# A four-layer graph network on one core: gathered rounds stand behind other dense units of a step

## The reference, cut to what matters

```
def sage_conv(x, src, dst, Wl, bl, Wr):
    msg = x[src]
    agg = jax.ops.segment_sum(msg, dst, num_segments=N_NODES)
    deg = jax.ops.segment_sum(jnp.ones((src.shape[0], 1), x.dtype), dst, num_segments=N_NODES)
    agg = agg / jnp.maximum(deg, 1.0)
    return agg @ Wl.T + bl + x @ Wr.T
...
edge_index = jnp.stack([src, dst])
x = _layernorm(x + _L0_gnn_ref(...), axis=-1)      # gat
x = _layernorm(x + _L1_gnn_ref(x, edge_index))     # dev: sums of x[src] and of its square
x = _layernorm(x + _L2_gnn_ref(x, edge_attr_64, src, dst, ...))   # gine
x = _layernorm(x + _L3_gnn_ref(x, edge_index, ...))               # sage1 .. sage4
```

## Time and profile before

| what | value |
|---|---|
| median of 3 runs | 10336.57 us (10336.55 to 10338.63) |
| the profiled execution's own time | 10338.73 us |
| its span | 10336.9 us, granted PE clock 0.819 of full speed |
| busy share of the span | PE 68%, PE weight loads 50%, DVE 46%, POOL 44%, ACT 18% |
| HBM | 1337.9 MB read, 225.0 MB written |

### The profile page before, as it was taken

One profiled execution on the slowest core, in us unless ns is written; L12 is line 12 of the kernel. 1 busy time (PEld: TensorE's weight loads), 2 busy tenths in 40 slices (PEclk: granted clock), 3 DMA queues, 4 the chain that ended last, 5 costly groups with the idle time before them and its releaser, 6 DMA issues.

```text
span 10336.9 us, 260758 instructions
## 1 busy us (share of the span) xinstructions
PE 7025.2 (68%) x70494; PEld 5117.6 (50%) x70495; DVE 4776.3 (46%) x12912; ACT 1865.3 (18%) x3800; POOL 4554.0 (44%) x4467
## 2 busy tenths in 40 slices
PE   5888778778735666666778866666676454555677
PEld 4666556556522221113454545665675454444676
DVE  4555555555468877774443333333232332222333
ACT  2333333332211334551000000000000000000000
POOL 3777656555410000004661045435554765553754
PEclk7899888888868988998889977777777776667788
DMA  3444333333310122335556665665566676556676
GB/s 68 95 94 92 83 89 83 82 80 72 74 49 25 75 87 112 137 135 172 165 172 183 179 207 194 208 217 178 204 223 207 220 273 212 199 201 228 205 253 228
DMA packets 973370, 1566.22 MB, mean 152 GB/s; under 512 B 499841, under 2 KB 621441, under 8 KB 966402
## 3 DMA queue, kind: packets, MB, share of 16 engines
q1 hardware_dynamic: 485762, 1244.14, 34.2%
q0 software_dynamic: 150016, 196.43, 9.4%
q10 hardware_dynamic: 337280, 122.87, 4.6%
HBM read 1337.91 MB, written 225.00 MB: 151 GB/s over the span
## 4 chain that ended last, share of the span: by engine, by line
PE 38%; issue 18%; DVE 15%; POOL 12%; DVEq 9%; DMA 6%; ACT 2%; ACTq 0%; SPq 0%; POOLq 0%
PE ps_turn L977 15%; POOL ARENA L662 12%; PE ps_out L824 6%; PE ps_turn L932 4%; DMA ARENA<-counts 3%; PE ps_pair L824 2%; DMA ARENA<-edge_attr 2%; PE ps_turn L797 2%; DVE ARENA L1766 2%; DVE ARENA L1764 2%; PE ps_turn L735 1%; PE ps_out L739 1%; DVEq L1771 1%; PE ps_pair L859 1%; PE ps_out L1014 1%
## 5 line engine op out<-in xcount | busy, mean ns | idle before, releaser
L977 PE MATMUL ps_turn<-ARENA 128*128 128x192 bf16 (+2 forms) x28812 | 2722.3, 261 | 708.7 <-DVE DSUM L1916 322.7
L977 PEld LDWEIGHTS ps_turn<-ARENA 128*128 128x128 bf16 x28812 | 2286.0, 105 | 1134.9 <-issue 824.1
L662 POOL DMA_INDIRECT ARENA<-table_sage,idx x1920 | 1866.9, 972 | 1510.0 <-issue 993.2
L662 POOL DMA_INDIRECT ARENA<-table_gat,idx x1568 | 1728.8, 1103 | 1054.9 <-DMA idx<-src_r 557.2
L932 PE MATMUL ps_turn<-ARENA 128*128 128x392 bf16 (+1 forms) x4204 | 1058.5, 356 | 676.3 <-DVE ARENA L1766 375.4
L662 POOL DMA_INDIRECT ARENA<-table_dev,idx x480 | 469.8, 979 | 1671.3 <-ACT idx L1177 1527.9
L1764 DVE TENSOR_SCALAR ARENA<-ARENA 128x784 bf16<-128x784 f16 (+1 forms) x2102 | 1007.2, 479 | 357.1 <-issue 230.9
L932 PEld LDWEIGHTS ps_turn<-ARENA 128*128 128x128 bf16 (+1 forms) x4204 | 332.4, 100 | 1402.3 <-issue 1357.7
L662 POOL DMA_INDIRECT ARENA<-table_gine,idx x480 | 469.8, 979 | 945.4 <-issue 691.3
L1159 ACT ACTIVATE ARENA<-ps_turn 128x784 f32 x784 | 646.1, 824 | 1077.5 <-PE ps_turn L932 1077.1
L1916 DVE TENSOR_REDUCE DSUM<-ps_turn 128x64 f32<-128x192 f32 (+2 forms) x686 | 263.6, 384 | 1171.0 <-PE ps_turn L977 1074.4
(11 more groups left out here) (303 smaller groups left out, 6913.7 us busy)
## 6 DMA issues: line engine op xcount, KB each, us to landing
ARENA<-counts SPq DMA_DIRECT2D x1764, 448.0 KB
counts<-ARENA SPq DMA_DIRECT2D x49, 3136.0 KB, 9.0
ARENA<-counts SPq DMA_DIRECT2D x588, 224.0 KB
ARENA<-dst_b SPq DMA_DIRECT2D x393, 256.0 KB
ARENA<-edge_attr ACTq DMA_DIRECT2D x392, 128.0 KB
ARENA<-table_sage,idx POOLq DMA_INDIRECT x1920
ARENA<-table_gat,idx POOLq DMA_INDIRECT x1568
nodes_dev<-table_rows ACTq DMA_DIRECT2D x14, 672.0 KB
```

Of the source, the lines that this page charges most:

```text
L662: pool.indirect_dma_start(ps["buf"][:, s, c, 0:ps["row"]], None, ps["table"][:, :], bass.IndirectOffsetOnAxis(idx[:, s, c:c + 1], 0)).then ...
L977: last = pe.matmul(ps_dense[half][:, 0:n], RING[:, b, :], XP[:, b, :], start=(b == PIECE_AT[pieces[0]]), stop=(j == pieces[-1] and b == PI ...
```

## The change

`begin_step` loads two numbers for a step in place of one: a `gain` and a first value of `share`. For a step with n rounds behind step 0, `gain` is (n-1) sixths (in 16.16) and `share` begins at 1 minus `gain`, so that the first round stands behind the first unit and the last behind the last, the others evenly between; a step with one round has it behind its first unit. Step 0 keeps its equal shares. The units behind which a round stands (counted from 0):

| step | rounds | before | after |
|---|---|---|---|
| 0 | 3 | 2, 4, 6 | 2, 4, 6 |
| 1 | 3 | 2, 4, 6 | 0, 3, 6 |
| 2 to 5 | 2 | 3, 6 | 0, 6 |
| 6 | 1 | 6 | 0 |

```diff
+LATER_SHARE = (1 << 16) // (TB - 1) + 1
...
-        GAINS = sb("GAINS", [P, STEPS], I32)
+        SHARES = sb("SHARES", [P, STEPS, 2], I32)
...
             gain, share, base, _, upto = turns
-            eng.reg_load([gain], GAINS[0:1, bass.ds(b, 1)])
-            eng.reg_mov(share, 0)
+            eng.reg_load([gain, share], SHARES[0:1, bass.ds(b, 1), :].rearrange("p a k -> p (a k)"))
             eng.reg_mov(base, upto)
...
-                gain = small[:, 2, 0:STEPS]
-                step(ve.tensor_tensor(gain, TARGETS[:, 1:STEPS + 1], TARGETS[:, 0:STEPS], ALU.subtract))
-                step(ve.tensor_scalar(gain, gain, float(TURN_SHARE), None, ALU.mult))
-                step(ve.tensor_copy(GAINS[:, :], gain))
+                rounds, gain, start = (small[:, q, 0:STEPS] for q in (2, 3, 4))
+                step(ve.tensor_tensor(rounds, TARGETS[:, 1:STEPS + 1], TARGETS[:, 0:STEPS], ALU.subtract))
+                step(ve.tensor_scalar(gain, rounds, -1.0, 0.0, ALU.add, ALU.max))
+                step(ve.tensor_scalar(gain, gain, float(LATER_SHARE), None, ALU.mult))
+                step(ve.tensor_scalar(start, rounds, 1.0, float(1 << 16), ALU.min, ALU.mult))
+                step(ve.tensor_tensor(start, start, gain, ALU.subtract))
+                step(ve.tensor_scalar(gain[:, 0:1], rounds[:, 0:1], float(TURN_SHARE), None, ALU.mult))
+                step(ve.memset(start[:, 0:1], 0.0))
+                step(ve.tensor_copy(SHARES[:, :, 0], gain))
+                step(ve.tensor_copy(SHARES[:, :, 1], start))
```

## The result

| | before | after |
|---|---|---|
| median of 7 runs each, on one chip | 10339.89 us (10336.55 to 10352.51) | 10387.46 us (10375.98 to 10408.45) |
| the profiled execution's span | 10336.9 us | 10394.3 us |

The ratio is 1.0047, with a 95% interval of 1.0036 to 1.0058: the changed kernel is slower by 47.6 us. The forecast was 10380 us.

The account below looks back on a forecast made before the run. Waits bound the kernel, no engine being busy over 68%; rounds end at least 41 to 42 us apart by gathers. Six passes +37.0 and `dev`'s load +6.3 make +43 on 10336.6: 10380 us, range 10357 to 10425 (0.68).

Parts of the forecast that it names:

- F: From a step's last round's end to the next step's first round's end: 41 us by gathers, 56.2 to 69.4 elsewhere.
- W: Six units in a row after a step's first round: 48.7 to 51 us by pass, sized from step 6 before.
- the two-round steps: Steps 2 to 5: F + 1.1 + W + 12.9, 103.7 to 134.4 us by pass; they lose, most in `sage2`.
- the last round in `dev`: Round ending a two-round step, its gathers already in hand: 12.9 us.
- Step 1: Three rounds, three units apart: F + 2 x 41.5, 124.0 to 152.4 us by pass; a gain in every pass.
- Step 6: One round behind unit 0: F + 1.1 + W, 90.8 to 121.5 us by pass.
- `dev`'s load: `XP` reload at the end of `dev`'s first half loses its covering round; PE waits 15 us bare, net +6.3 us.
- The cover is needed: One-hots made inside first rounds delay PE 5.5 us in `gine`, `sage3`, 4.5 in `sage1`; rival, not needed: 10287 us, chance 0.14.
- given back in `sage2`: Rival: after waiting, PE runs six units 6.7 us faster per step, total 10340; chance 0.12 shared with another place.
- The rounds stand where the change puts them: Rival: rounding of `share` puts the first round behind unit 1, about 10340; chance 0.12 shared with the wait given back.
- DVE's node work holds the gathers back: Rival: rounds waiting for gathers beside node work end later than 41 us, up to 10623 in all; chance 0.06.
- the 8 us ahead of `more_hots`: Sign of being right: behind unit 0, `more_hots` some 8 us after the unit's first sum, four one-hots between.

Follow-up runs that it names:

- one unit later: Against the kernel before: rounds of steps 2 to 5 behind units 1 and 6, other steps as before; 10349.35 us, ratio 1.0011.

## Why the prediction was right

**F was right in size, and in two of the six passes by luck.** The first round of a step ends 41.9, 68.8, 54.5, 40.8, 57.7 and 41.4 us after the last one (`dev` to `sage4`, means of six steps); forecast were 41, 69.4, 56.2, 41, 57.6 and 41. In `sage2` the cause is shown by halving the gathers, in `gine`, `sage1` and `sage3` by doubling the one-hots. In `dev` and `sage4` the prediction let the round end with its gathers "whatever PE does". But PE waits there for DVE, 69.3 and 65.1 us for `tile_hots` beside 4.1 and 11.4 for gathered rows; half the gathers take only 1.0 and 1.7 us off F, and four more one-hots add 2.8 and 2.0. With half the gathers no first round there waits for rows in steps 2 to 5, so DVE's node work and one-hots take some 40.9 and 39.7 us by themselves; that this lies next to 41 was not foreseen. In `gine`, `sage1` and `sage3` the sum held two errors that cancelled: a round without waits lasts 12.6 to 13.0 us there and not 11, and a first round is longer than that by 3.3, 2.2 and 3.5 us and not 5.5, 4.5 and 5.5. The 3.47 us that the earlier trace rows show ahead of `more_hots` are not spent a second time.

**W was mis-sized.** Six units in steps 2 to 5 take 48.9, 53.9, 52.7, 48.5, 49.0 and 53.3 us; forecast were 50, 51, 51, 48.7, 48.7 and 51. The term came from step 6, where no gathers run in `gine` and `sage3`. Beside gathers it is longer, and with half of them it falls back to 51.5, 51.5, 47.0, 46.9 and 51.4 in `gine` to `sage4` (`dev` stays at 49.2). Over four steps the six differences make some 24 us, and the two-round steps exceed the forecast by 24.0; the last round in `dev`, 14.1 us where 12.9 were taken, adds some 5, and `sage1`'s shorter F takes some 6 back. So `gine` and `sage4`, forecast to gain 4.5 and 2.8 us in their stretches, lost 2.1 and 8.3.

**Step 1** gained 71.1 us where 63.7 were forecast: behind its first round the last of the other two ends 81.0 to 83.4 us later, 83 had been taken. **Step 6** lost 27.4, forecast 29.4.

**`dev`'s load** stands bare for 14.94 us as said, and the gap of 6.5 us behind the 50th unit is gone; +6.3 was forecast, and from there to `gine` it is +4.4. What was not in the sum is the 7.2 us that the later passes' ends give back.

**The rivals.** The cover is needed (87 us for four more one-hots). Nothing is given back in `sage2`: its six units take 48.5 us, as forecast, and not 42. The rounds stand where the change puts them. And DVE's node work holds the gathers back only a little: from a step's last round to the next one's first a gather follows the one before after 1.34 us in `dev` and 1.31 in `sage4`, in place of 1.25, some 1.5 and 1.1 us over the 17 or 18 gathers there (the prediction allowed 0.6), and F is within 1.1 us of `sage2`. The rule of the Trainium skill, SBUF — State Buffer, section "SBUF: two separate sides", as the prediction took it, is about DVE's two-port modes. Which of the operations here ran in one the trace does not tell, so it neither bears the rule out nor refutes it; what did not come is the rival's size, all of DVE's busy time taken from POOL.

**The total** came out 47.6 us by medians where 43 were forecast: 14.6 too little in the stretches, and on the other side 7.2 not foreseen at the passes' ends and 1.9 too much for `dev`'s load; the rest is within what single runs differ by. That it came so near owes something to luck: W alone is some 24 us too small, and step 1 and the passes' ends, 7 us better each, hide more than half of that. Of the signs that the prediction named for being right, the 8 us ahead of `more_hots` did not come (5.45); of those for being wrong, none did.

## What to carry to other kernels

Work that hides behind a supplier with a fixed pace wants the supplier's period on both sides, counted in time and not in places: here 41 us of gathers need four units between two rounds, or the node work with units: three in `sage2`, two in the other passes (with two, in "one unit later", PE waits for rows in the first rounds of steps 2 to 5 in `sage2` alone, 19.5 us). Even spacing by index is not even spacing in time when the ends of a step hold other work. And a stretch that is to size a term must have the same transfers beside it as the one that it stands for.

## Not expected of the hardware

POOL's time for gathers here hangs on the number of indirect DMAs and hardly on their rows: 932 ns for one with 64 rows, 965 with 128, a pitch of some 1.25 us, and F in `sage2` went from 40.8 to 39.2 us only.

A gather lasts longer beside DVE. In the changed kernel's six passes 1074 gathers ran while DVE stood idle: 0.944 us on the mean, none over 0.961. Another 420 ran beside one-hot operations alone: 1.026 on the mean, up to 1.480. Here is one of them in `sage2`, DVE's row and POOL's:

```profile
8280.98 2.74 DVE L1849 SCALAR_TENSOR_TENSOR ARENA<-DST,TBASE,COL 128x512 f32 x4 [2.82 <-issue]
8281.99 1.22 POOL L662 DMA_INDIRECT ARENA<-table_sage,idx  x1 [0.31 <-issue]
```

No run tried what the two share.

Six dense units, which don't touch the gathers' data, take 1.7 to 2.8 us more with 26 or 27 gathers beside them than with none, in `gine` at the same granted clock. That the gathers cause it is shown by halving their number; through which resource was not tried.
